# Means of two batches in a row in the second cross-attention, and expert places read twenty at a time

## What is computed

```python
def _moe_forward(x, router_w, router_b, w1, b1, w2, b2, top_k=2):     # layer 3: E = 8 experts, H = 512
    logits = jnp.einsum('bsd,de->bse', x, router_w) + router_b
    top_vals, top_idx = jax.lax.top_k(logits, top_k)
    ...
    h = jax.nn.relu(jnp.einsum('td,edh->eth', xf, w1) + b1[:, None, :])
    y = jnp.einsum('eth,ehd->etd', h, w2) + b2[:, None, :]
    out = jnp.einsum('etd,te->td', y, gf)

def _L1_xattn_ref(x, latents, mask, Wq, Wkv, Wout, bout, g_media, b_media, g_latent, b_latent):   # layer 4
    xn = layer_norm(x, g_media, b_media)              # x: the context, 64 x 257 x 128
    ln = layer_norm(latents, g_latent, b_latent)      # 64 x 32 x 128
    q = (ln @ Wq).reshape(B, Q, NUM_HEADS, DIM_HEAD).transpose(0, 2, 1, 3) * scale    # 16 heads of 64
    kv_input = jnp.concatenate([xn, ln], axis=1)      # 257 + 32 = 289 keys
    ...
    sim = jnp.where(full_mask[:, None, None, :], max_neg, sim)
    alphas = jax.nn.softmax(sim, axis=-1)
    out = jnp.einsum('bhqf,bhfv->bhqv', alphas, v)
    out = out.transpose(0, 2, 1, 3).reshape(B, Q, HIDDEN)
    return out @ Wout + bout
```

## Time and profile before

| | us |
|---|---|
| median of 3 runs | 1157.24 (1157.15 to 1159.02) |
| the profiled execution | 1159.96 |
| its span in the profile | 1158.2 |
| loop of experts, first to last L1174 | 428 to 551 |
| second cross-attention, first scores to last output added | 585.06 to 988.41 |

### The profile page before, as it was taken

How to read it: one execution, slowest core, us unless ns; L and a number is a source line. 1 busy time by engine, 2 the same in 40 slices (tenths; PEclk the granted TensorE clock), 3 DMA queues, 4 the chain that set the end, 5 groups by cost and what they waited for, 6 DMA issues and landing times. The chain is left out here.

```text
span 1158.2 us, 38099 instructions
## 1 busy us (share of the span) xinstructions
PE 1014.6 (88%) x13865; PEld 804.5 (69%) x13868; DVE 742.8 (64%) x2792; ACT 748.8 (65%) x1794; POOL 484.1 (42%) x883
## 2 busy tenths in 40 slices
PE   5899999986787867878899999999999998886864
PEld 2678888854676657767578888888888887422343
DVE  3678888865788478887366565565565564464376
ACT  2688888853687437666367666666666664564467
POOL 1122222215453046556056666666666665113042
PEclk9899999998899879999999999999999999999979
DMA  2543333300000726663374444444454442000001
GB/s 61 129 110 81 81 81 80 79 18 0 1 1 1 296 65 188 193 188 109 98 185 130 114 129 115 120 126 123 116 129 118 118 129 68 28 0 1 0 1 38
DMA packets 70701, 105.60 MB, mean 91 GB/s; under 512 B 12560, under 2 KB 50320, under 8 KB 70384
## 3 DMA queue, kind: packets, MB, share of 16 engines
q1 hardware_dynamic: 68080, 98.84, 31.5%
q0 software_dynamic: 2496, 5.12, 1.7%
HBM read 89.12 MB, written 14.79 MB: 90 GB/s over the span
## 5 line engine op out<-in xcount | busy, mean ns | idle before, releaser
L1716 DVE CUSTOM_DVE_ANT_0 d_p<-bank,d_low 128x289 f32<-128x289 f32 x256 | 110.2, 431 | 105.9 <-PE bank L1604 105.8
L1681 ACT ACTIVATE d_p<-d_p,d_nmax 128x289 f32<-128x289 f32 x256 | 137.4, 537 | 62.2 <-DVE d_nmax L1716 56.3
L1552 POOL TENSOR_TENSOR d_p<-d_p,d_rtotal 128x288 f32<-128x288 f32 x256 | 167.6, 667 | 11.7 <-DVE d_rtotal L1722 11.3
L1604 PE MATMUL bank<-x_keyT,d_q 128*128 128x289 f32 x512 | 154.4, 422 | 2.4 <-DVE d_nmax L1716 1.3
L1730 DVE STREAM_TRANSPOSE d_pT<-d_p 128x288 f32<-128x288 f32 x256 | 120.0, 469 | 55.2 <-POOL d_p L1552 49.2
L1618 PE MATMUL bank<-d_pT,d_xr 32*128 32x128 f32 x4608 | 146.6, 276 | 0.0
L1618 PEld LDWEIGHTS bank<-d_pT,d_xr 32*128 32x128 f32 x4608 | 134.4, 187 | 9.0 <-issue 1.9
L445 ACT ACTIVATE a_p<-a_p,a_nmax 128x257 f32<-128x257 f32 x256 | 116.2, 506 | 31.3 <-DVE a_nmax L482 29.6
L482 DVE CUSTOM_DVE_ANT_0 a_p<-bank,a_low 128x257 f32<-128x257 f32 x256 | 93.8, 422 | 25.5 <-PE bank L395 23.5
L1604 PEld LDWEIGHTS bank<-x_keyT,d_q 128*128 128x128 f32 x512 | 83.2, 189 | 31.5 <-DVE d_nmax L1716 16.1
L353 POOL TENSOR_TENSOR a_edge<-a_vlast,a_p 128x32 f32<-128x32 f32 x64 | 15.8, 246 | 173.9 <-ACT a_p L445 160.7
(11 more groups left out here) (344 smaller groups left out, 2217.2 us busy)
## 6 DMA issues: line engine op xcount, KB each, us to landing
d_xr<-key_rows SPq DMA_DIRECT2D x256, 144.0 KB, 2.9
d_low<-mask_low SPq DMA_DIRECT2D x64, 144.5 KB, 3.3
a_ctT<-in_ctxT SPq DMA_DIRECT2D x64, 128.5 KB, 2.1
a_low<-mask_low SPq DMA_DIRECT2D x64, 128.5 KB, 3.0
c_ct<-in_ctx SPq DMA_DIRECT2D x32, 256.0 KB
key_rows<-c_ct SPq DMA_DIRECT2D x32, 256.0 KB
c_w<-in_L_ffn_w SPq DMA_DIRECT2D x8, 578.0 KB, 10.5
c_w<-expert_out SPq DMA_DIRECT2D x8, 256.0 KB, 4.4
```

Source lines behind the costliest of these rows:

```text
L1552: nc.gpsimd.tensor_tensor(p, p, rtotal[:, b % 2, g:g + 1].broadcast_to([128, EDGE]), ALU.mult).then_inc(normed, 1)
L1604: nc.tensor.matmul(S[u % 2], q[:, b // 4, b % 4, 4 * g:4 * g + 4, :].rearrange("p h q -> p (h q)"), keyT[:, bass.ds(i * EIGHT + b, 1), :]. ...
L1681: nc.scalar.activation(p, p, ACT.Exp, bias=nmax[:, b % 2, g:g + 1], scale=-1.0, accum_out=total[:, b % 2, g:g + 1]).then_inc(exp_made, 1)
L1716: nc.vector.tensor_tensor_reduce(P[:, b % 2, g, 0:KEYS], S[u % 2], low[:, b % 4, :], -1.0, 3.4e38, ALU.add, ALU.min, accum_out=nmax[:, b % ...
```

## The change

In the second cross-attention:

- PE does the means of two batches in a row, at every odd batch, of the batches n - 3 and n - 2; each has columns of its own in banks 2 to 5 (0:256 and 256:512), pT has four slots, and the two parts of the means have two slots each, in memory that another stage owns. The wait for `o_copied` is made once for a pair.
- ACT copies the means of two batches (n - 4, n - 3) at every even batch, after its four exponentials, and copies the queries after the second exponential instead of after the fourth.
- POOL combines two batches (n - 5, n - 4) at every odd batch, ahead of its first `normalise`.
- `project` is two batches later, on PE and on DVE, whose addition moves to the batches with b % 4 == 0; the end has eight parts of it instead of six, around the last pair of means.
- SP issues the rows of two batches at every odd batch, and each mask ahead of them.

In the experts: both reads take twenty places at a time (before slots 0 and 20) and leave out the check of the bounds at run time.

```diff
@@ experts_0
-    DEEP = 4
+    DEEP, PLACES = 4, 20
...
-                if s % 4 == 0 and s < SLOTS:
-                    _, values = nc.values_load_multi_w_load_instructions(weight_at[0:1, s:s + 4], engines=(mybir.EngineType.PE,), min_val=0, max_val=(E - 1) * WIDTH)
-                    at.update(zip(range(s, s + 4), values))
+                if s % PLACES == 0 and s < SLOTS:
+                    _, values = nc.values_load_multi_w_load_instructions(weight_at[0:1, s:s + PLACES], engines=(mybir.EngineType.PE,), min_val=0, max_val=(E - 1) * WIDTH,
+                                                                         skip_runtime_bounds_check_because="an expert is a count of at most E - 1 first tiles, times WIDTH")
+                    at.update(zip(range(s, s + PLACES), values))
...
-                if (s + 1) % 4 == 0 and s + 1 < SLOTS:
+                if (s + 1) % PLACES == 0 and s + 1 < SLOTS:
                     load_places(s + 1)
@@ cross_attention_1, sync
+                    if b >= 2:
+                        mask(0, b + 2)
+                    if b % 2 == 1:
+                        rows(0, b - 1, b < 2)
+                        rows(0, b, b < 2)
@@ cross_attention_1, gpsimd
                     for u in range(UNITS):
                         b, g = divmod(u, GROUPS)
+                        n = i * EIGHT + b
+                        if g == 0 and b % 2 == 1 and n >= 5:
+                            combine(n - 5)
+                            combine(n - 4)
                         normalise(i, u)
-                        if g == 0 and i * EIGHT + b >= 2:
-                            combine(i * EIGHT + b - 2)
@@ cross_attention_1, tensor
-                    if not first:
+                    if n % 2 == 0 and n >= 2:
                         pe.wait_ge(o_copied, 2 * n)
...
-                            ins = nc.tensor.matmul((OL if latents else O)[j], xr[rows, b % 2, k, :], pT[rows, b % 2, :, 32 * k:32 * k + 32],
+                            ins = nc.tensor.matmul((OL if latents else O)[n % 2][j], xr[rows, n % 2, k, :], pT[rows, n % 4, :, 32 * k:32 * k + 32],
...
-                    ago, r = divmod(b - 6, 4)
+                    ago, r = divmod(b - 8, 4)
...
-                        if not (first and b < 6):
+                        if not first:
                             project(i, b)
-                        if not (first and b == 0):
-                            means(i, b - 1, first and b == 1)
+                        n = i * EIGHT + b
+                        if b % 2 == 1 and n >= 3:
+                            means(n - 3)
+                            means(n - 2)
...
-                project(TURNS, 0)
-                project(TURNS, 1)
-                means(TURNS, -1)
-                for r in range(4):
-                    project(TURNS, 2 + r)
+                for r in range(3):
+                    project(TURNS, r)
+                means(BATCH - 2)
+                means(BATCH - 1)
+                for r in range(3, 8):
+                    project(TURNS, r)
@@ cross_attention_1, scalar
                         for g in range(GROUPS):
                             exponential(i, b * GROUPS + g)
-                        if not (last and b >= 4):
-                            queries(i, b)
-                        if not (first and b == 0):
-                            means(i, b - 1)
+                            if g == 1 and not (last and b >= 4):
+                                queries(i, b)
+                        n = i * EIGHT + b
+                        if b % 2 == 0 and n >= 4:
+                            means(n - 4)
+                            means(n - 3)
@@ cross_attention_1, vector
-                    if g == 0 and not (first and b < 2):
-                        dve.wait_ge(o_made, i * EIGHT + (b - 1))
-                    nc.vector.transpose(pT[:, b % 2, g, :], P[:, b % 2, g, 0:EDGE]).then_inc(turned, 1)
+                    if g == 0 and not (first and b < 4):
+                        dve.wait_ge(o_made, i * EIGHT + (b - 3))
+                    nc.vector.transpose(pT[:, b % 4, g, :], P[:, b % 2, g, 0:EDGE]).then_inc(turned, 1)
...
-                        if b % 4 == 2 and g == 1 and not first:
-                            project(i, (b - 10) // 4)
+                        if b % 4 == 0 and g == 1 and i * EIGHT + b >= 12:
+                            project(i, (b - 12) // 4)
```

More of the change, by code:

```diff
@@ L1428, in load_places @@
             def load_places(s):
-                _, values = nc.values_load_multi_w_load_instructions(weight_at[0:1, s:s + 4], engines=(mybir.EngineType.DVE,), min_val=0, max_val=(E - 1) * WIDTH)
-                at.update(zip(range(s, s + 4), values))
+                _, values = nc.values_load_multi_w_load_instructions(weight_at[0:1, s:s + PLACES], engines=(mybir.EngineType.DVE,), min_val=0, max_val=(E - 1) * WIDTH,
+                                                                     skip_runtime_bounds_check_because="an expert is a count of at most E - 1 first tiles, times WIDTH")
+                at.update(zip(range(s, s + PLACES), values))
             load_places(0)
@@ L1486, in cross_attention_1 @@
         nmax, total, rtotal = (sb(f"d_{n}", [128, 2, GROUPS]) for n in ("nmax", "total", "rtotal"))
-        a, latent_part, context_part = sb("d_a", [128, 2, HEADS, 4, LAT]), *(sb(f"d_{n}_part", [128, 4, 128]) for n in ("latent", "context"))
+        a, (latent_part, context_part) = sb("d_a", [128, 2, HEADS, 4, LAT]), (core.out[:, n:n + 8, :].rearrange("p (e j) c -> p e j c", e=2) for n in (0, 8))
         S = [core.bank[:, n, 0:KEYS] for n in (0, 1)]
-        O, OL = ([core.bank[:, 2 + j, n:n + 128] for j in range(4)] for n in (0, 128))
+        O, OL = ([[core.bank[:, 2 + j, n + at:n + at + 128] for j in range(4)] for n in (0, 256)] for at in (0, 128))
         FIRST_Q, OUT = [core.bank[:, n, :] for n in (6, 7, 0, 1)], core.bank[:, 7, 0:128]
@@ L1527, in _ @@
                 for b in range(EIGHT):
-                    rows(0, b, b < 2)
+                    if b >= 2:
[3 more added lines that the diff above has]
+                        rows(0, b, b < 2)
                     if b == 1:
@@ L1532, in _ @@
                             sp.dma_start(last_values[32 * j:32 * j + 32], cx.last_dram.rearrange("(i b) (g j) d -> j (b g) i d", i=TURNS, j=4)[j]).then_inc(cx.last_loaded, 16)
-                    if b >= 2:
-                        mask(0, b + 2)
-                for i in range(1, TURNS - 1):
+                for i in range(1, TURNS):
                     for b in range(EIGHT):
[L1537 to L1542, removed]
+                        if i * EIGHT + b + 2 < BATCH:
+                            mask(i, b + 2)
+                        if b % 2 == 1:
+                            rows(i, b - 1)
+                            rows(i, b)
             @block.gpsimd
@@ L1574, in body @@
                         b, g = divmod(u, GROUPS)
+                        n = i * EIGHT + b
+                        if g == 0 and b % 2 == 1 and n >= 5:
+                            combine(n - 5)
+                            combine(n - 4)
                         normalise(i, u)
-                        if g == 0 and i * EIGHT + b >= 2:
-                            combine(i * EIGHT + b - 2)
                 pool.wait_ge(cleared, 1)
                 unrolled(TURNS, body)
-                combine(BATCH - 2)
-                combine(BATCH - 1)
+                for n in range(BATCH - 4, BATCH):
+                    combine(n)
             @block.tensor
@@ L1605, in scores, with means @@
                                      keyT[:, bass.ds(i * EIGHT + b, 1), :].rearrange("p a k -> p (a k)"), start=True, stop=True).then_inc(s_made, 1)
-                def means(i, b, first=False):
-                    n = i * EIGHT + b
-                    pe.wait_ge(xr_loaded[b % 2], (i * (EIGHT // 2) + b // 2) * 64 + 64)
+                def means(n):
+                    pe.wait_ge(xr_loaded[n % 2], (n // 2) * 64 + 64)
                     pe.wait_ge(turned, (n + 1) * GROUPS)
-                    if not first:
+                    if n % 2 == 0 and n >= 2:
                         pe.wait_ge(o_copied, 2 * n)
@@ L1682, in exponential, with means @@
                                          accum_out=total[:, b % 2, g:g + 1]).then_inc(exp_made, 1)
-                def means(i, b):
-                    n = i * EIGHT + b
-                    act.wait_ge(o_made, n + 1)
-                    if n >= 1:
-                        act.wait_ge(a_made, n)
-                    nc.scalar.activation(latent_part[:], core.bank[:, 2:6, 128:256], ACT.Identity, bias=affine[:, 1:2]).then_inc(o_copied, 1)
-                    nc.scalar.activation(context_part[:], core.bank[:, 2:6, 0:128], ACT.Copy, scale=affine[:, 0:1]).then_inc(o_copied, 1)
+                def means(n):
+                    at, part = 256 * (n % 2), n % 2
+                    act.wait_ge(o_made, n - n % 2 + 2)
+                    if n >= 2:
```

(7 more changed lines are left out.)

6 lines of the change are left out of this document (3 added, 3 removed).

## The result

The changed kernel takes 1138.73 us (median of 4 runs, 1137.29 to 1140.5) against 1157.2 for the kernel before: ratio 0.9864, 95% interval 0.983 to 0.9898. Two later comparisons, each with both kernels on one chip, gave 0.9878 (0.9853 to 0.9904) and 0.9873 (0.9851 to 0.9895), that is 14.2 and 14.6 us. The forecast was 1142, 15.4 us less. The total is right; its two parts are not (one was too small and the other too large), and what decides the larger of them was not seen.

What follows compares the result with a forecast made beforehand. PE, never idle, was taken to bound the second cross-attention; late `down` results were taken to set the experts' time. From 1157.24, cross-attention -10.4 and experts -5.0 gave 1141.8, said as 1142; range 1131 to 1155, 8 in 10.

Steps and rivals of the forecast that it cites:

- The late results of `down`: Experts: DVE adds `down` 3.2 us late in every second slot, read or not, so a removed read saves only 0.56 us.
- Rival 2: Experts: late results vanish with the reads, slots run at DVE's 2.72 us, 21 us gained instead of 4.5, total 1126; chance 0.10.
- The price of a read: Experts: one load of 0.568 us and four times 0.148 + 0.018 of check, 1.23 us on PE and DVE.
- the load of twenty places: Experts: each remaining read costs between one load of 0.57 and five, 2.84 us; -0.5 us taken for both.
- Cross-attention: Second cross-attention: means in pairs halve PE's mode changes, 0.49 us saved per two batches; stage -10.4 us, bounds -13.2 and -4.8.
- 144 x 0.0267 + 0.30: Cross-attention: PE's time for a pair of means, weight loads plus the change back to whole-array work, 4.14 us.
- The first four batches: Cross-attention's start: four batches without means, paced by DVE, 16th scores done at 597.95, first pair of means ending at 602.2.
- The two pairs without a project: Early cross-attention: the copies hold the means back, 7.24 + 4.14 = 11.38 us for each pair.
- The sixth scores' stall: Cross-attention: DVE's addition beside the last keys' transpose delays the fourth maximum, stalling PE 0.20 us in every second pair.
- rival 1: Cross-attention: DVE and ACT hold PE 0.4 us per pair at the seventh and eighth scores, stage gains nothing, 1152.7; chance 0.15.
- rival 3: Cross-attention: ACT's four copies end 1.5 us late, PE's means wait 1.0 us in each of 28 pairs, 1171; chance 0.08.
- rival 4: PE drains between a pair's two means too, and registers cost by the piece so experts gain nothing: about 1155; chance 0.07.

Runs made afterwards that it cites:

- experts alone: Kernel before with only the experts' reads changed (twenty places, no bounds check), cross-attention as before: 1161.72 us, ratio 0.9967, on one chip; 1146.71 us, 0.994, on another.

## Why the forecast was right in the sum, and where its steps were not

**The late results of `down`: the step that failed.** "It is late in every second slot, with a read or without" was true of the execution shown, and I read it as something the kernel does in every run, so that a removed read was worth 0.56 us. Two kernels show otherwise: the same experts' part has a loop of 118.0 us on chip A and 102.4 on C, and before has 122.1 in the profile shown and 113.0 on C. So of the 19.9 us between the first two profiles 10.6 are the change and some 9 are late results that the one execution had and the other hadn't. Where the results are late, the size of the step is right: on A the experts' part gained 3.8 us, and 4.7 in the loop (forecast 5.0, bounds 1.5 to 6). Where they are not, eight removed reads are worth 10.6 us in the loop instead of 4.5, 1.3 each and not 0.56. Rival 2, at 0.10, had half of it: slots of 2.73 throughout, but no cause in the reads, and a price of 21 us that counted the late results too.

**The price of a read.** I took 1.23 us, from PE's instructions. VectorE's register operation takes 0.186 us where PE's takes 0.148, and VectorE is the engine that paces a slot (busy 2.69 of 2.72 us). The run in which only PE's reads are changed shows that PE's are worth nothing (112.8 on chip B against 113.0 on C). I also gave the check no price apart from the load; it is 8.0 of the 10.6. For the load of twenty places the forecast had 0.57 to 2.84 us; it is 1.60. The Trainium skill's floor of about 600 ns (DMA: Bandwidth & Descriptors, Latency and other measured facts) agrees with the median of 0.58; as a floor it doesn't hold, since the shortest load of four places took 0.34 in the same rows. Its about 200 ns for each register even in bulk (Runtime: NRT & Kernel Launch, Instruction fetch mechanics, said of loads from HBM) doesn't hold for this load from on-chip memory: (1.60 - 0.58) / 16 = 0.064 us for each further place.

**Cross-attention: mechanism right, size 6.1 instead of 10.4 us, inside the bounds.** Most of the pair's timetable came true: means in one run of 144, the fourth maximum at 3.91 (forecast 3.92), the copies 0.52 us ahead of the means (forecast 0.5), the last keys' product in every second pair. Four terms make the difference of 4.3:
- Pairs take 12.07 and 12.12 instead of 12.01 and 12.03, 2.0 us over 28. The pair of 12.12 has no idle time at all; its pieces sum to that. The means with the way back to whole-array work take 4.23, not the 4.14 of my 144 x 0.0267 + 0.30.
- The first four batches take 3.3 to 3.6 us each, 13.8 up to the first means where I had 12.9: +0.9.
- The two pairs without a project take 11.66 and 11.46, not 11.38: +0.4.
- The last pair's means wait for their rows, which I had called hidden: +0.8 in the first profile and +1.0 on chip C (the rows below); the three projects ahead of them and the way through the means add 0.2.

```profile
948.85 2.94 PE L1635 MATMUL bank<-d_a,x_wvo 128*128 128x128 f32 x24
952.67 4.30 PE L1622 MATMUL bank<-d_pT,d_xr 32*128 32x128 f32 x144 [0.88 <-DMA d_xr<-key_rows]
```

SP now issues a pair's rows only behind the means that free the buffers. In the middle of the stage 8 us remain for that; at the end, where three projects are all that lies between the last two pairs of means, they don't. This last cause was read from the trace, not tried.

**The sixth scores' stall.** It is there, at the forecast's size (1.16 us from the sixth scores' pair to the queries at 636.41 to 637.57, instead of 0.98). Its cause was only half right: moving the sum out of that unit saved 0.03, since POOL's `normalise` is late there anyway.

**Rivals 1, 3 and 4.** PE's weight loads wait 0.17 us for maxima outside the sixth scores in nearly all pairs (0.74 in a few), which costs the 12.12 pair nothing: rival 1 didn't happen. The means never waited for the copies in a pair with a project: rival 3 didn't happen. No step at the 72nd load, and registers that cost 0.064 each: rival 4 didn't happen. The slip that would have made the kernel slower was none of them but the place of the queries' copy, which the change had right.

**What no step had.** The last group's projection, the same 32 matmuls, took 3.84 us or 5.2 to 5.5, by the granted clock: 1.00 throughout (2.4 GHz) in the short ones, 0.69 to 0.76 as the mean of the stretch in the long ones, so for a part of it at the lower level. PE sat idle 2.6 to 2.7 us ahead of it in both cases, so that idle time alone doesn't decide it. Busy time by stretch (PE, PEld, DVE, ACT, POOL, granted clock, DMA), the changed kernel, then before, both on chip C:

```profile
961.00:966.20 5.20, 5.20 (x33) 5.20 (x34) 0.00 (x0) 0.00 (x0) 0.00 (x0) 0.69 0.00 0
```

```profile
979.00:983.00 4.00, 3.82 (x34) 3.63 (x33) 0.14 (x1) 0.00 (x0) 0.00 (x0) 1.00 0.00 0
```

That is 1.6 us lost here. In the first two profiles it was 1.4 gained: 5.21 us for its 32 matmuls before, at a granted clock of 0.72 to 0.76, and 3.84 after, at 1.00. And 1.6 to 2.0 us of the experts' gain are given back between the loop and the first scores. The loop's 10.6 and the stage's 6.1 less these 1.6 to 2.0 give 14.7 to 15.1 us; the side-by-side medians differ by 14.2 and 14.6. The 2.8 us by which the first `up` started earlier on chip C are not the change's: the experts' part alone, with the same instructions up to there, started it at 429.5, as late as the kernel before (429.9). So the forecast of 15.4 had one part 5.6 us too small and the other 4.3 too large; that the two errors nearly cancel is luck, and the total says nothing for either step.

## What to carry to other kernels

Before a wait in one profile is built into a sum, ask whether the kernel causes it: a result that is late in every second slot turned out to belong to some executions and not to others, and the experts' part of the forecast hung on it. Price a step by the engine that paces the loop, not by the one whose row is easiest to find, and price its assertions apart from its load. When two pieces of work are pushed together, look for every buffer that relied on the distance between them; here one copy of 0.58 us, in the wrong place, cost more than the whole change gained.

## What the hardware showed that was not expected

- TensorE's results were signalled late through a whole loop in all four runs on one chip and in none of eight on two others, one kernel with the same instructions among both (experts alone). In the profile of experts alone on chip A PE's records go on at their usual pace from the `down` that ends at 443.04 to the transpose that ends at 445.88, 2.8 us of work, and the trace's semaphore events have the signals of all that work between 446.06 and 446.37; ACT and DVE start right behind the first ones, at 446.12 and 446.20. So it is the signals that come late and not the work. The granted clock there is 1.00, and between 440 and 540 us it is 0.98 in both profiles of the kernel before, of which only the first has late results. The cost is 9 to 16 us in this loop (before: 122.1 and 113.0; experts alone: 118.0 and 102.4). What holds the signals stays open; no run here separates it, nor the chip from the time at which it was used.
- Twenty places are loaded into registers in 1.60 us, four in 0.58; checking one costs VectorE 0.21 us, or 0.28 with its gaps, three to four times the 0.064 of loading one more.
